# X's rows of 1040 bytes in place of 1056 in a graph attention layer, the low half beginning at byte 520 in place of 528

## The reference

```python
in_fts = context @ W_common.T
left   = in_fts @ w_left + b_left
right  = in_fts @ w_right + b_right
logits = left[:, None] + right[None, :]
logits = where(logits >= 0, logits, 0.2 * logits)
logits = where(adj <= 0.0, -inf, logits)
coefs  = softmax(logits, axis=-1)
x      = layernorm(x + relu(coefs @ x))
```

## Time and profile before

| | |
|---|---|
| median of 3 runs | 1478.76 us (1478.73 to 1478.93) |
| the profiled execution, its own time | 1475.81 us |
| its span, first to last instruction | 1474.0 us |
| mean granted TensorE clock | 0.970 |
| TensorE, matmul | 1375.1 us busy, 93% |
| VectorE | 1300.5 us busy, 88% |
| ScalarE | 642.9 us busy, 44% |
| GpSimd | 88.6 us busy, 6% |

### The profile page before, as it was taken

One profiled execution on the slowest core, in us unless ns is written; L12 is line 12 of the kernel. 1 busy time (PEld: TensorE's weight loads), 2 busy tenths in 40 slices (PEclk: granted clock), 3 DMA queues, 4 the chain that ended last, 5 costly groups with the idle time before them and its releaser, 6 DMA issues.

```text
span 1474.0 us, 28321 instructions
## 1 busy us (share of the span) xinstructions
PE 1375.1 (93%) x12334; PEld 1206.2 (82%) x12334; DVE 1300.5 (88%) x1140; ACT 642.9 (44%) x675; POOL 88.6 (6%) x215
## 2 busy tenths in 40 slices
PE   1049899999999999999999999999999999999998
PEld 0026788888888888888888888888888888888887
DVE  6979899898998899898989989898998989899981
ACT  0386444544444354444435444444445444444441
POOL 0007000000000000000000000000000000000000
PEclk7569999999999999999999999999999999999999
DMA  9995998989898998989999898999999898999860
GB/s 385 353 246 147 242 238 224 228 209 239 206 246 213 230 226 217 230 215 235 214 235 219 222 233 211 236 214 236 223 225 226 210 243 209 235 221 219 209 170 9
DMA packets 180752, 329.59 MB, mean 224 GB/s; under 512 B 19728, under 2 KB 36112, under 8 KB 179600
## 3 DMA queue, kind: packets, MB, share of 16 engines
q1 hardware_dynamic: 177264, 321.47, 87.9%
q10 hardware_dynamic: 3360, 6.29, 1.3%
HBM read 319.29 MB, written 8.39 MB: 222 GB/s over the span
## 4 chain that ended last, share of the span: by engine, by line
PE 88%; DMA 4%; DVE 3%; ACT 2%; POOL 2%; issue 1%; SPq 1%; ACTq 0%; POOLq 0%; DVEq 0%
PE ps L397 29%; PE ps L398 29%; PE ps L399 29%; DVE tab L564 2%; DMA T<-in_L_gnn_context_dram 1%; DMA T<-in_x_dram 1%; ACT X L435 1%; POOL X L302 1%; DMA strip<-in_adj_dram 1%; POOL xs L298 1%; ACT strip L464 1%; DVE T L755 0%; SPq L209 0%; ACTq L214 0%; DVE tab L547 0%
## 5 line engine op out<-in xcount | busy, mean ns | idle before, releaser
L397 PE MATMUL ps<-X,T 128*128 128x257 f16 x3968 | 1084.0, 273 | 3.8 <-DVE T L755 3.8
L399 PE MATMUL ps<-X,T 128*128 128x257 f16 x3968 | 1084.1, 273 | 0.0
L398 PE MATMUL ps<-X,T 128*128 128x257 f16 x3968 | 1084.0, 273 | 0.0
L464 ACT ACTIVATE strip<-strip 128x2048 f32<-128x2048 f32 x256 | 489.0, 1911 | 504.7 <-DMA strip<-in_adj_dram 503.3
L711 DVE SCALAR_TENSOR_TENSOR strip<-tab,arow,strip 128x2048 f32<-128x2048 f32 x256 | 598.1, 2337 | 57.1 <-ACT strip L464 56.1
L755 DVE STREAM_TRANSPOSE T<-strip 128x2048 f32<-128x2048 f32 x256 | 590.1, 2306 | 58.8 <-PE ps L399 58.6
L397 PEld LDWEIGHTS ps<-X,T 128*128 128x128 f16 x3968 | 390.0, 98 | 52.4 <-DVE T L755 4.1
L399 PEld LDWEIGHTS ps<-X,T 128*128 128x128 f16 x3968 | 388.5, 98 | 48.4
L398 PEld LDWEIGHTS ps<-X,T 128*128 128x128 f16 x3968 | 388.5, 98 | 48.1
L445 ACT ACTIVATE xs<-ps,small 128x256 f32<-128x256 f32 x64 | 30.3, 473 | 139.8 <-DVE small L760 139.6
L308 POOL TENSOR_SCALAR small<-small 128x1 f32<-128x1 f32 x64 | 12.3, 192 | 1261.6 <-ACT xs L453 1261.6
(11 more groups left out here) (94 smaller groups left out, 283.3 us busy)
## 6 DMA issues: line engine op xcount, KB each, us to landing
strip<-in_adj_dram SPq DMA_DIRECT2D x1016, 256.0 KB, 4.8
xs<-in_L_gnn_context_dram SPq DMA_DIRECT2D x14, 1024.0 KB, 9.3
T<-in_L_gnn_context_dram SPq DMA_DIRECT2D x4, 2048.0 KB, 16.6
X<-in_L_gnn_context_dram SPq DMA_DIRECT2D x4, 2048.0 KB, 32.9
xs<-in_x_dram SPq DMA_DIRECT2D x64, 128.0 KB, 5.4
out_dram<-xs SPq DMA_DIRECT2D x64, 128.0 KB, 5.2
gw<-in_L_gnn_context_dram SPq DMA_DIRECT2D x2, 1024.0 KB, 19.2
strip<-in_adj_dram ACTq DMA_DIRECT2D x8, 256.0 KB, 12.6
```

What stands on the lines that cost most here:

```text
L397: nc.tensor.matmul(ps[o][:, 0:D + 1], hi, X16[:, jb, 0:D + 1], start=(jb == 0), stop=False)
L398: nc.tensor.matmul(ps[o][:, 0:D + 1], hi, X16[:, jb, XL:XL + D + 1], start=False, stop=False)
L399: m = nc.tensor.matmul(ps[o][:, 0:D + 1], lo, X16[:, jb, 0:D + 1], start=False, stop=(jb == JB - 1))
L464: nc.scalar.activation(s, s, ACT.Relu, scale=KEEP).then_inc(s_m, 1)
```

## The change

One constant of the row's layout is smaller by 4. Since `XW = XL`, it sets both the start of the low half, in float16 elements, and the length of a row, in float32 words:

```diff
     NS = N // B
     SG = P // B
     NG = N // P
-    XL = D + 8
+    XL = D + 4
     XW = XL
     NB = 4
     NY = 4
```

## The result

| | before | after |
|---|---|---|
| median | 1478.22 us (6 runs) | 1485.93 us (6 runs) |
| profiled execution, its own time | 1475.81 us | 1486.32 us |
| its span | 1474.0 us | 1484.5 us |

The ratio is 1.0052, with a 95% interval of 1.0042 to 1.0062: 7.7 us, with 6.2 to 9.2. The time lies inside the stated range of 1476 to 1493 us, but the forecast of no change, 1478.8 us, was wrong: the kernel is slower, about half as much as the first rival said. One of the ten executions of the kernel with X shifted by 16 bytes, further down, took 8302 us and is not in its ratio.

What follows compares the result with a forecast made beforehand. The prediction took TensorE's matmul count by the distance between starts to bound the kernel. All terms were 0: 1475.81 + 0 = 1475.8 us profiled, and 1478.8 us from the median of before; range 1476 to 1493 us.

Steps and rivals of the forecast that it cites:

- the first rival: TensorE's low-half reads (L398): a misaligned start costs one more step of 3.4 ns, +13.3 us, 1492.1 us; chance 0.20.
- What bounds the kernel: Main loop: from 175.77 us to the last matmul, time is the number of matmuls by their starts' distance, 0.110 us.
- High rows at 16 beyond a multiple of 32: TensorE's high-half reads, 2 of 3 matmuls: they take places of a kind low rows had before, cost 0.
- Low rows: TensorE's low-half reads, 3904 matmuls of L398, now at 8 beyond 16: taken as 0, ends +13.3 and -11.3 us.
- The reading of the half clock: Stretch at granted 0.50: 214.5 ns a step, taken as 257 columns and no more, so the fetch has room.
- A low half fetched twice: TensorE's low reads: every piece fetched twice doubles a low matmul, 429 us more, 1908 us; chance 0.03.
- GpSimd's writes: Setup, L302: a write at 8 mod 16 doubles it, 15.0 us pass down the chain, 1493.8 us; chance 0.03.
- the lone element (faster): Low reads' last 16-byte block: its single element costs 2.9 ns, which goes away, -11.3 us, 1467.5 us; chance 0.06.
- The setup: Writes of X ahead of the main loop by GpSimd, ScalarE and VectorE: each taken as 0, ends up to 1.7 us.
- ScalarE's: Setup, ScalarE's writes of 256 float16 in 494 to 500 ns: taken as 0, with an end of 0.8 us.

Runs made afterwards that it cites:

- the octets: Changed kernel with the products of eight blocks ordered 8 high, 8 low, 8 high; 1478.09 us against 1477.77 us for the kernel before, ratio 1.0003.
- the pairs: Changed kernel with two neighbouring blocks' products ordered high, high, low, low, high, high; 1482.14 us against 1478.40 us for the kernel before, ratio 1.0026.

## Where the prediction was right and where it was wrong

- **What bounds the kernel: right.** Time is the number of matmuls by the distance of their starts, and the change of that distance is all of the change of time: 3904 x 2.08 ns = 8.1 us for a measured 7.7.
- **High rows at 16 beyond a multiple of 32, "cost 0, shown": right** in itself; shifted by 16 bytes, everything still steps by 110.0.
- **Low rows, "I take 0": this step failed.** They were the one unknown on the path, and it measured +3.75 ns on their own step, -0.83 on each of the other two, +2.08 a block. The argument counted blocks touched by a single read, 33 either way. The count is right, and the free shift of all by 8 fits it; it looked at each read alone, and the cost arises between two successive ones, the high read that ends at byte 513 and the low one that begins at 520.
- **The reading of the half clock misled.** The 214.5 ns were worked out from starts of two decimals; to the nanosecond the same 11 steps take 2.366 us, 215.1 ns each, and 12 of them 215.0, so the matmul did not pay for "its 257 columns and no more" (214.2) but for one column's time beyond them. And that it paid for little more than its columns was taken to mean that the fetch has room. The changed kernel also has 215.0 ns there, as before, so the half clock could not have shown this cost.
- **The rival "a misaligned low half costs a step"** had the place right (L398 to L399 at 113 ns, measured 113.75, about 4500 matmuls in 500 us, measured 4524), and the long step of 3.4 was sized well at 3.75. Its mechanism was wrong, since the shift of all by 8 costs nothing, and its sum of +13.3 us too large, since it forgot that neighbours can give time back. The forecast range was drawn up to this rival and so held the result, 1485.93 us. That was luck in part: it held the time by a mechanism that the runs refute, and the chance given to a slower kernel was 0.26 against 0.68 for no change.
- **A low half fetched twice, GpSimd's writes, and the lone element (faster): wrong**, the first by 113.75 ns for the low step, the second by L302's 2141 ns, and the third by both the 113.75 ns and the 109.2 ns of the low step with 256 columns. The Trainium skill's page "TensorE: Matmul & The Clock Gate", section "Wait — 56ns, not 53.3ns?", gives a fixed addition of about 2.5 ns per warm matmul and does not speak of where a read starts. An estimate from it is 109.6 ns for 257 columns: the trace has 110.0 in the kernel before, 0.4 more, and 113.75 for the low reads of the changed kernel, which disagrees.
- **The setup: right,** every term 0 within 8 ns per instruction; ScalarE's, which moved most, became shorter.

## What to carry to other kernels

Where matmuls follow each other without a gap, the distance between their starts is worth reading to the nanosecond: 2 ns a block were 0.5% of this kernel, while no busy share moved by more than a point. If two operands read one behind the other are packed into one row, it was free here to let the second start outside the 16 bytes of its predecessor's last element (528 behind 513, 528 behind 521), or to read another block in between, as the octets do; whether that is the whole rule was not tested. Starts that are merely off a 16-byte boundary cost nothing here. Ask of an address change not only what each read does alone, but what follows what: the order of eight blocks' products gave the shorter rows, 1024 bytes a partition saved, at the time of before (ratio 1.0003).

## What was not expected of the hardware

- Matmul reads of X that begin 8 bytes off a 16-byte boundary run at the full pace, 110.0 ns for 257 columns, when all do. (X's own start is taken as a multiple of 16 bytes.)
- After a long step the next matmuls are shorter than the steady 110.0: 109.2 ns, three of them behind the one of 112.4 ns in the octets, which makes the time even; behind the 114.2 ns of the pairs it does not become even. So 110.0 is not the least distance between these matmuls.
- The extra time of a low half at 514 to 524 exists at the granted clock of 1.00 (2.4 GHz) alone; at 0.50 (1.2 GHz) the kernel before, the changed one and those at 514, 516, 520 and 524 all step by 215.0 ns.
- One column less, 256 in place of 257, shortened a step by 0.8 ns at 2.4 GHz, twice a column's time, and 257 columns at 1.2 GHz took 215.0 ns, the time of 258.
